# Mamba stage: the scan's decay in PSUM, and B's rows brought by DMA from a DRAM scratch

## The reference

```python
xz = x @ W_in + b_in
x_proj, z = jnp.split(xz, 2, axis=-1)                 # 256 channels each
xa = silu(causal_conv(x_proj, 4 taps) + conv_b)
dtBC = xa @ W_xp + b_xp
dt_int, B_c, C_c = jnp.split(dtBC, [DT_RANK, DT_RANK + D_STATE], axis=-1)   # 16, 16, 16
dt = softplus(dt_int @ W_dt + b_dt)
A = -exp(A_log)
# for each time step t, h of [channel, 16 states], from 0
A_bar = exp(dt_t[..., None] * A)
h = A_bar * h + dt_t[..., None] * B_t[:, None, :] * x_t[..., None]
y_t = sum(C_t[:, None, :] * h, axis=-1)
...
y = (y + xa * D_ssm) * silu(z) @ W_out + b_out
```

## Time and profile before

| | |
|---|---|
| median of three runs | 6530.44 us |
| profiled execution | 6521.4 us |
| its span, first to last instruction | 6519.7 us |
| TensorE's granted clock, mean of the span | 0.909 |
| the Mamba stage's 128 scans | start at 91.3 to 775.7 us |
| busy in 85 to 785 us: scans L2918 on VectorE | 395.1 us, mean 3087 ns |
| the same: drive L2740 on GpSimd | 350.6 us, mean 2747 ns |
| the same: read L2925 on VectorE | 156.2 us, mean 1221 ns |
| the same: decay L2859 on ScalarE | 217.4 us, mean 496 ns |
| the same: copies of B L2851 on ScalarE | 73.9 us, mean 578 ns |

### The profile page before, as it was taken

One profiled execution on the slowest core, in us unless ns is written; L12 is line 12 of the kernel. 1 busy time (PEld: TensorE's weight loads), 2 busy tenths in 40 slices (PEclk: granted clock), 3 DMA queues, 4 the chain that ended last, 5 costly groups with the idle time before them and its releaser, 6 DMA issues. The chain is left out here.

```text
span 6519.7 us, 133036 instructions
## 1 busy us (share of the span) xinstructions
PE 5408.8 (83%) x51329; PEld 3520.5 (54%) x51329; DVE 4462.5 (68%) x7059; ACT 3417.4 (52%) x5825; POOL 2692.6 (41%) x1600
## 2 busy tenths in 40 slices
PE   7889755897789888888888888888888887996866
PEld 4444322454566666665666666666666664663233
DVE  5888889575677767777777777777777775674222
ACT  4565422454556556655566555565556664552123
POOL 2565411000455545554555555555555552660000
PEclk8888866898999999999999999999999998996857
DMA  1000000000000000000000000100010000000000
GB/s 30 0 0 0 4 0 0 6 2 5 28 11 10 25 14 11 10 25 14 10 11 25 15 10 11 28 10 11 11 28 10 12 10 12 2 2 7 12 1 16
DMA packets 69221, 72.82 MB, mean 11 GB/s; under 512 B 20856, under 2 KB 51528, under 8 KB 68048
## 3 DMA queue, kind: packets, MB, share of 16 engines
q1 hardware_dynamic: 60624, 67.88, 4.2%
q10 hardware_dynamic: 8256, 0.03, 0.1%
HBM read 28.06 MB, written 2.10 MB: 5 GB/s over the span
## 5 line engine op out<-in xcount | busy, mean ns | idle before, releaser
L2147 POOL TENSOR_TENSOR lt_qk<-lt_qk,lt_rot 128x1024 f32<-128x1024 f32 x384 | 905.4, 2358 | 560.2 <-DVE lt_rot L2501 560.2
L2157 POOL TENSOR_TENSOR lt_prob<-lt_prob,lt_total 128x1024 f32<-128x1024 f32 x192 | 365.3, 1903 | 1247.4 <-DVE lt_total L2527 1240.6
L2196 PE MATMUL lt_ps<-lt_w_qk,lt_xs 128*128 128x512 f32 x1536 | 773.9, 628 | 74.3 <-issue 52.9
L2152 POOL TENSOR_TENSOR lt_qk<-lt_qk,lt_rnorm 128x1024 f32<-128x1024 f32 x384 | 728.3, 1908 | 58.9 <-ACT lt_rnorm L2375 51.2
L2247 PE MATMUL lt_ps<-lt_z,lt_fold 128*128 128x256 f32 x3072 | 681.0, 380 | 1.1 <-ACT lt_z L2403 1.1
L2368 ACT ACTIVATE lt_sq<-lt_ps 128x1024 f32<-128x1024 f32 x384 | 393.4, 1025 | 521.5 <-PE lt_ps L2196 513.6
L2247 PEld LDWEIGHTS lt_ps<-lt_z,lt_fold 128*128 128x128 f32 x3072 | 585.1, 191 | 122.3 <-ACT lt_z L2403 24.6
L2498 DVE TENSOR_TENSOR lt_qk<-lt_ps,lt_table 128x1024 f32<-128x1024 f32 x384 | 466.1, 1214 | 191.6 <-ACT lt_sq L2368 187.3
L2501 DVE TENSOR_TENSOR lt_rot<-lt_ps,lt_table 128x512 f32<-128x512 f32 x768 | 488.8, 675 | 0.0
L2508 DVE TENSOR_REDUCE lt_norm<-lt_sq 128x16 f32<-128x1024 f32 x384 | 463.7, 1208 | 1.8 <-ACT lt_log L2372 0.3
L2740 POOL TENSOR_TENSOR mb_drive<-mb_u,mb_bs 128x1024 f32<-128x1024 f32 x128 | 350.6, 2747 | 275.8 <-ACT mb_bs L2851 155.6
(11 more groups left out here) (439 smaller groups left out, 11041.0 us busy)
## 6 DMA issues: line engine op xcount, KB each, us to landing
lt_xw<-lt_xw SPq DMA_DIRECT2D x192, 128.0 KB
lt_xs<-h SPq DMA_DIRECT2D x96, 64.0 KB, 1.9
lt_w_qk<-in_L_ffn_Wqkv SPq DMA_DIRECT2D x6, 1024.0 KB, 5.1
lt_xs<-h SPq DMA_DIRECT2D x96, 63.8 KB, 2.0
lt_wvT<-in_L_wvT SPq DMA_DIRECT2D x6, 512.0 KB, 7.2
lt_wo<-in_L_ffn_Wo SPq DMA_DIRECT2D x6, 512.0 KB, 8.3
out<-xo SPq DMA_DIRECT2D x8, 256.0 KB, 2.7
lt_w<-in_L_ffn_W SPq DMA_DIRECT2D x6, 341.0 KB, 3.1
```

The lines of the kernel that those rows point to most:

```text
L2147: pool.tensor_tensor(qk[:, u, :, :], qk[:, u, :, :], rot[:, u % 2, :, :], ALU.add).then_inc(sg["added"], 1)
L2152: pool.tensor_tensor(qk[:, u, :, :], qk[:, u, :, :], rnorm[:, u, :, :].to_broadcast([P, H, DH]), ALU.mult).then_inc(sg["qk"], 1)
L2196: last = pe.matmul(AT[u][:, 512 * k:512 * k + 512], xs[:, m.j, c:c + P], w_qk[:, a, 512 * k:512 * k + 512], start=True, stop=True)
```

## The change

1. `decay` moves from SBUF to PSUM: four of the eight banks. To make room `ps_z` and `ps_c` become one bank, `ps_n` (C's rows) goes from two buffers to one, and `ps_b` goes. Position 0 of each run is zeroed by a memset on VectorE after the layer norm (which now uses decay's banks), and ScalarE waits for it before the first item.
2. B's rows are no longer spread by TensorE and copied by ScalarE. In g = 4 SyncE writes the 16 rows of the next item (`bcd[0:N]`, 16 KB) to a DRAM scratch `mb_rows`, waits, and reads them back with a source that repeats for each of the 128 partitions: first 4 rows (`b_soon`, 512 KB written to SBUF), then 12 (`b_late`, 1536 KB). `bs` now holds a whole item, twice.
3. C's rows are spread in the group that uses them, after the read of the group before (one buffer). The convolution is split over g = 1 and g = 2, z's projection moves from g = 0 to g = 2, and the output's bias on ScalarE from g = 2 to g = 1.

```diff
-    BC = 2 * N
-    assert CT == 2 and BC == 32
+    ROW_C, ROW_DT = 32, 64
+    assert CT == 2 and N <= ROW_C and R <= ROW_C
...
-        bs = sb("bs", [P, 2, 1, 2, S])
-        decay = sb("decay", [P, 2, CT, 2, S])
+        bs = sb("bs", [P, 2, 1, N, S])
+        rows = nc.dram_tensor("mb_rows", [2, N * S], F32).ap()
         drive = sb("drive", [P, 2, CT, 2, S])
...
-        ps_z = psum("ps_z", [P, CT, S])
-        ps_c = psum("ps_c", [P, 2, S])
-        ps_b = psum("ps_b", [P, 2, 1, 2, S])
-        ps_n = psum("ps_n", [P, 2, 1, 2, S])
+        ps_z = psum("ps_z", [P, 2, S])
+        ps_n = psum("ps_n", [P, 1, 2, S])
         ps_y = psum("ps_y", [P, CT * S])
-        ln.ps_mean = ps_b[:, :, 0, :, :].rearrange("p j k s -> p j (k s)")
-        ln.ps_var = ps_n[:, :, 0, :, :].rearrange("p j k s -> p j (k s)")
-        LOADS = 16
+        decay = psum("decay", [P, 2, CT, 2, S])
+        halves = decay[:, :, :, :, :].rearrange("p j t k s -> p j t (k s)")
+        ln.ps_mean, ln.ps_var = halves[:, 0, :, :], halves[:, 1, :, :]
...
+        LOADS = 15
+        SOON = 4
...
+        def run(eng, ahead, here, phase, back):
+
+
+            def item(n, j, more=True):
+                first = isinstance(n, int) and n == 0
+                for g in range(G):
+                    if g < G - 1:
+                        ahead(n, j, g + 1)
+                    elif more:
+                        ahead(n + 1, 1 - j, 0)
+                    here(n, j, g)
+                    if not first:
+                        back(n - 1, 1 - j, g)
+                    if more:
+                        phase(n + 1, 1 - j, g)
+
+            for g in range(G - 1):
+                phase(0, 0, g)
+            ahead(0, 0, 0)
+            pairs(eng, B - 2, item)
+            item(B - 2, 0)
+            item(B - 1, 1, more=False)
+            for g in range(4):
+                back(B - 1, 1, g)
...
+            sp.wait_ge(sg["const"], 4)
+            sp.dma_start(w_xp[:, :, 0:N], w_bc[:, :, R:R + N]).then_inc(sg["w_in"], 16)
...
+            def phase(n, j, g):
+                if g == 4:
+                    sp.wait_ge(sg["bcd"], n + 1)
+                    sp.sem_inc(sg["rows_step"], 1)
+                    if not (isinstance(n, int) and n == 0):
+                        sp.wait_ge(sg["drive"], G * (n - 1) + SOON)
+                        sp.sem_inc(sg["rows_step"], 1)
+                    sp.dma_start(rows[j:j + 1, :].rearrange("a (n s) -> (a n) s", n=N), bcd[0:N, j, :]).then_inc(sg["rows"], 16)
+                    sp.wait_ge(sg["rows"], 16 * (n + 1))
+                    for name, low, high in (("b_soon", 0, SOON), ("b_late", SOON, N)):
+                        sp.dma_start(bs[:, j, 0, low:high, :].rearrange("p n s -> p (n s)"),
+                                     rows[j:j + 1, S * low:S * high].to_broadcast([P, S * (high - low)])).then_inc(sg[name], 16)
+
+            run(sp, idle, idle, phase, idle)
...
-            pool.memset(decay[:, :, :, :, :], 0.0).then_inc(sg["const"], 1)
+            pool.memset(w_xp[:, :, :], 0.0).then_inc(sg["const"], 1)
+            pool.memset(b_xp[:, :], 0.0).then_inc(sg["const"], 1)
...
-                pool.wait_ge(sg["b_copied"], G * n + g + 1)
+                if g == 0:
+                    pool.wait_ge(sg["b_soon"], 16 * (n + 1))
+                if g == SOON // 2:
+                    pool.wait_ge(sg["b_late"], 16 * (n + 1))
                 wait(pool, sg["scanned"], G * n + g - 1)
                 pool.tensor_tensor(drive[:, g % 2, :, :, :], u[:, j, :, :, :].to_broadcast([P, CT, 2, S]),
-                                   bs[:, g % 2, :, :, :].to_broadcast([P, CT, 2, S]), ALU.mult).then_inc(sg["drive"], 1)
+                                   bs[:, j, :, 2 * g:2 * g + 2, :].to_broadcast([P, CT, 2, S]), ALU.mult).then_inc(sg["drive"], 1)
...
-            def ahead(n, j, g):
-                wait(pe, sg["read"], G * n + g - 1)
-                for k in range(2):
-                    last = pe.matmul(ps_n[:, g % 2, 0, k, :], sel[BC:2 * BC, 2 * g + k, :], bcd[BC:2 * BC, j, :], start=True, stop=True,
-                                     tile_position=(BC, 0))
-                last.then_inc(sg["c_spread"], 1)
-
-            def far(n, j, g):
+            def spread(n, j, g):
                 if g == 0:
                     pe.wait_ge(sg["bcd"], n + 1)
-                wait(pe, sg["b_copied"], G * n + g - 1)
+                wait(pe, sg["read"], G * n + g)
                 for k in range(2):
-                    last = pe.matmul(ps_b[:, g % 2, 0, k, :], sel[0:BC, 2 * g + k, :], bcd[0:BC, j, :], start=True, stop=True,
-                                     tile_position=(0, 0))
-                last.then_inc(sg["b_spread"], 1)
+                    last = pe.matmul(ps_n[:, 0, k, :], sel[ROW_C:, 2 * g + k, :], bcd[ROW_C:ROW_C + N, j, :], start=True, stop=True,
+                                     tile_position=(ROW_C, 0))
+                last.then_inc(sg["c_spread"], 1)
...
+                spread(n, j, g)
...
-                    wait(pe, sg["silu_z"], n)
-                    for t in range(CT):
+                if g in (1, 2):
+                    t = g - 1
+                    pe.wait_ge(sg["x"], n + 1)
+                    for k in range(TAPS):
+                        last = pe.matmul(ps_a[:, t, :], taps[:, k, t, :], xpad[:, t, k:k + S], start=(k == 0), stop=(k == TAPS - 1))
+                    last.then_inc(sg["conv"], 1)
+                if g == 2:
+                    wait(pe, sg["biased"], n - 1)
+                    wait(pe, sg["bcd"], n)
+                    for t in range(2):
...
-                if g == 1:
-                    pe.wait_ge(sg["x"], n + 1)
-                    for t in range(CT):
-                        for k in range(TAPS):
-                            last = pe.matmul(ps_a[:, t, :], taps[:, k, t, :], xpad[:, t, k:k + S], start=(k == 0), stop=(k == TAPS - 1))
-                    last.then_inc(sg["conv"], 1)
...
-                    wait(pe, sg["biased"], n - 1)
+                    pe.wait_ge(sg["silu_z"], n + 1)
                     for t in range(CT):
-                        last = pe.matmul(ps_c[0:2 * BC + R, 1, :], w_xp[:, t, :], cz[:, j, t, :], start=(t == 0), stop=(t == CT - 1))
+                        last = pe.matmul(ps_z[0:ROW_DT + R, 1, :], w_xp[:, t, :], cz[:, j, t, :], start=(t == 0), stop=(t == CT - 1))
...
+            act.wait_ge(sg["first_zero"], 1)
...
-            def far(n, j, g):
-                act.wait_ge(sg["b_spread"], G * n + g + 1)
-                wait(act, sg["drive"], G * n + g - 1)
-                act.copy(bs[:, g % 2, 0, :, :], ps_b[:, g % 2, 0, :, :]).then_inc(sg["b_copied"], 1)
...
-                    act.wait_ge(sg["conv"], n + 1)
+                    act.wait_ge(sg["conv"], 2 * n + 2)
...
-                if g == 2:
+                if g == 1:
                     act.wait_ge(sg["out"], n + 1)
                     wait(act, sg["added"], n - 1)
-                    nc.scalar.activation(tmp[:, j, :], ps_c[:, 0, :], ACT.Identity, bias=b_out[:, 0:1]).then_inc(sg["biased"], 1)
+                    nc.scalar.activation(tmp[:, j, :], ps_z[:, 0, :], ACT.Identity, bias=b_out[:, 0:1]).then_inc(sg["biased"], 1)
...
+            dve.wait_ge(sg["ln_log"], B // 2)
+            nc.vector.memset(decay[:, :, :, :, :], 0.0).then_inc(sg["first_zero"], 1)
...
-                                        ps_n[:, g % 2, :, :, :].to_broadcast([P, CT, 2, S]), ALU.mult).then_inc(sg["read"], 1)
+                                        ps_n[:, :, :, :].to_broadcast([P, CT, 2, S]), ALU.mult).then_inc(sg["read"], 1)
```

More of the change, by code:

```diff
@@ L2689, in _ @@
                 sp.dma_start(b_out[:, :], T["L0_attn_b_out"].rearrange("(p a) -> p a", a=1)).then_inc(sg["w_in"], 16)
-                for c in range(2):
-                    sp.dma_start(b_xp[BC * c:BC * c + BC, :], b_bc[R:R + BC, :]).then_inc(sg["w_in"], 16)
-                sp.dma_start(b_xp[2 * BC:, :], b_bc[0:R, :]).then_inc(sg["w_in"], 16)
-        def run(eng, ahead, far, here, phase, back):
-            def item(n, j, more=True):
-                first = isinstance(n, int) and n == 0
-                for g in range(G):
-                    if g < G - 1:
-                        ahead(n, j, g + 1)
-                    elif more:
-                        ahead(n + 1, 1 - j, 0)
-                    if g < G - 2:
-                        far(n, j, g + 2)
-                    elif more:
-                        far(n + 1, 1 - j, g + 2 - G)
-                    here(n, j, g)
-                    if not first:
-                        back(n - 1, 1 - j, g)
-                    if more:
-                        phase(n + 1, 1 - j, g)
-            for g in range(G - 1):
-                phase(0, 0, g)
-            far(0, 0, 0)
-            ahead(0, 0, 0)
-            far(0, 0, 1)
-            pairs(eng, B - 2, item)
-            item(B - 2, 0)
-            item(B - 1, 1, more=False)
-            for g in range(4):
-                back(B - 1, 1, g)
```

(10 more changed lines are left out.)

34 lines of the change are left out of this document (19 added, 15 removed).

## The result

The changed kernel took 6382.88 us in the median (6378.85 to 6385.12, 4 runs), the kernel before beside it 6529.17 us (6524.81 to 6532.07). Its profiled execution took 6383.19 us, its span 6381.5, so profile against profile the gain is 138.2 us.

What follows compares the result with a forecast made beforehand. Mamba is bound by scan and drive excluding each other (groups 5 to 7) and TensorE (groups 0 to 4). 14 x (43.3 - 37.5) = 81, plus 3 and 7, less 2, saves 89 us: 6530.4 - 89 = 6441 us, range 6410 to 6475.

Steps and rivals of the forecast that it cites:

- The exclusion: Mamba groups 5 to 7: VectorE's scan (2.28 us) and GpSimd's drive (2.36) cannot overlap; decay in PSUM ends this.
- The surcharge for a PSUM source: Mamba's scans: by the skill's larger fixed PSUM cost, 128 scans would take 8 us more; left out of the sum.
- the pair of the earlier trace: Layer norm: instructions with a PSUM input (681 ns) and two SBUF inputs (697 ns), taken to show PSUM costs nothing.
- ScalarE into PSUM: Mamba's decay activations: four writes to PSUM taken as 1.70 us as now, between 1.5 and 2.2.
- two cases: Mamba item bounded by TensorE: 36.0 us at full clock, 38.3 to 39.4 if the low level follows its wait; 37.5 taken.
- One sign asked for: Mamba item: TensorE without waits from g = 0 to g = 4 would show the forecast right.
- B's spread: Mamba, TensorE: lies beside C's spread in time, so removing it saves TensorE nothing.
- DMA: Mamba, B's rows: write at most 2.7 us, then 2048 KB in 10.2; both parts hidden, b_late with 7 us to spare.
- The rival of late B: Mamba: the repeated DRAM read is slow, b_late lands 15 us late, items take 51 to 52 us; 6655 us, chance 0.08.
- Ends: Mamba's ends: last item saves 3 us, item 0 saves 7 (3 to 10), 2 lost before the first scan.
- TensorE did not stay slow: Rival in Mamba: TensorE's clock stays low, items take 40 to 41 us; 6485 us, chance 0.18 shared with slow scan.
- the exclusion did not stay: Rival in Mamba: exclusion goes with the scan's instruction, only drives' waits for copies go; 6522 us, chance 0.06.

Runs made afterwards that it cites:

- the six traces named above: Traces of runs with decay in PSUM and the out projection in its old place, group 1; Mamba's pitch 37.06 to 37.52 us an item.
- a shift of 240: Changed kernel with out projection moved to group 5, plus 240 effectless semaphore increments on TensorE ahead of the local transformer: 6671.84 us, ratio 1.0215.
- the shift of the table: Effectless TensorE instructions ahead of the local transformer, 0 to 240, counted from the changed kernel (kernel before stands at 123): 6382.88 to 6671.84 us.
- two runs: Changed kernel with 123 and with 192 effectless increments on TensorE ahead of the local transformer: 6439.59 and 6543.35 us.
- a third: Changed kernel with out projection in group 5, 72 increments ahead of the local transformer and 52 between its two loops: 6368.4 us, ratio 0.9772.

## Why the prediction was wrong, and where it was right

The time was missed by 58 us (6441 against 6382.88). Against the profile, where the working was done, it is 6521.4 - 89 = 6432.4 against 6383.19, so 49.2: 1.2 in Mamba (90.2 saved instead of 89), 47.6 in the local transformer, 0.4 elsewhere. The other 9 us are the distance of the median from the profile, 9.0 before, which I carried over; after, the two agree to 0.3 us.

- *What bounds it, and the scan.* Right. The exclusion came from two SBUF inputs: the scan's median is 2.28 us and its maximum 2.29 (under 2.6 was asked), no drive is over 2.36, and with decay in SBUF all of it comes back. The surcharge for a PSUM source, which I left out, is not there. But the pair of the earlier trace rows was a weak reason for leaving it out: the 681 ns are a subtraction (`cen`) and the 697 ns a multiplication (`h`). And the 8 us that the prediction works out by the Trainium skill's figure, on top of 6441, would make 6449, not 6446.
- *ScalarE into PSUM.* Taken as 1.70 us for four; it is 1.67 (374.20), 462 ns each against 496.
- *TensorE.* 36.0 us at full clock, 38.3 to 39.4 if low clock follows the wait, 37.5 taken; measured 37.33, and 37.06 to 37.52 over the six traces named above. The wait came as laid out, 2.14 us (2.2 foreseen), and the low level did follow it, but only over one sum. So the value was right by a compromise between two cases, and the case was a third; that it came so close is luck. One sign asked for is there: in the item at 392.85 to 419.74 us TensorE has no wait from g = 0 to g = 4.
- *B's spread* "saves TensorE nothing": true of time beside C's spread, which takes 1.06 us alone now (388.19 to 389.25) and 1.07 with B's before. The decay in SBUF run leaves 1.9 us an item to B's rows, the copies and the new order together, which I had not split.
- *DMA.* Write 1.4 us (2.7 allowed), 7.7 for the large part (10.2 for both): hidden, and hidden when doubled. The rival of late B is out. The figures that the prediction takes from the Trainium skill, "DMA: Bandwidth & Descriptors", section on the anatomy of one DMA, are fitted there for transfers that GpSimd issues, and these come from SyncE; the write's 1.4 us are under the fixed 2.0.
- *Ends.* Last item 31.69 us against 33.99, 2.3 saved (3 forecast; in others of the six traces the last item takes as little as 28.6); item 0 from 49.8 to 45.8, 4.0 saved (7 forecast, 3 the lower bound); before the first scan 0.2 won (2 lost forecast: the memset is there, ScalarE waits 3.8 us in its place, but the first scan starts no later). With 14 x 5.98 = 83.7 that is 90.2.
- *The rivals.* TensorE did not stay slow (0.94 where 0.85 was), the exclusion did not stay, B did not come late. None of the three was what happened.

The step that failed is the first sentence of the working: "The change touches the Mamba stage alone, so I read that stage only". It is true of the program's lines and not of its time. The change removes instructions from a queue whose code is loaded in blocks, and everything behind it moves. The long branches were there to be read in the profile before, as idle time with no releaser ahead of the loop's first projection (at the end of the row: idle us, and of it "issue"). Before and after:

```profile
L2196 PE MATMUL lt_ps<-lt_w_qk,lt_xs 128*128 128x512 f32 x1536 | 773.9, 628 | 74.3 <-issue 52.9
```

```profile
L2196 PE MATMUL lt_ps<-lt_w_qk,lt_xs 128*128 128x512 f32 x1536 | 759.1, 617 | 54.9 <-issue 33.2
```

That row says that the stage has something to win or to lose by a shift, though not which. From the 16 items a layer in all six layers, the time from the first item's start to the last's is 3774.2 us before, 3727.8 after and 4000.4 at a shift of 240: the sum lacked a term for this stage, which the runs show from -46 us to +226.

## What to carry to other kernels

Before a forecast that ends with "the rest is unchanged", look at the backward branches of the engine with the most instructions: if some take 0.2 us and others over 3, any edit that changes the number of instructions ahead of the loop can move the time by more than the edit's own worth, and a comparison of two versions should compare that stage too. A gain of a tuned kernel is only attributed once the untouched stages have the same length in both traces, and a few increments of an unused semaphore are a cheap way to test, or to repair, such a placement. And a VectorE instruction that fights with GpSimd's can be freed by moving one of its inputs to PSUM, at no cost in its own time here.

## What the runs showed of the hardware

- A backward branch on TensorE took 0.21 us with its target loaded and 3.3 to 5.1 us without, and each long one came with about nine more 16 KB packets of the instruction queue. Counting the place of each loop over items by the shift of the table (the last layer's plus 141), none was long at the places tried from 0 to 77, a third or half at 123 to 141, all from 173 to 240. Why these are the limits is open.
- After a long branch's 2.9 us of idleness TensorE worked at 1.2 GHz for the next 3.78 us of projection (1.88 at full clock).
- An increment of a semaphore costs TensorE's queue 0.155 us: 10.7 us for 69 of them between two runs, 8.1 us for 52 in a third.
- TENSOR_TENSOR_SCAN on 128x1024 f32 takes 2.28 us from one PSUM and one SBUF input, the same as undisturbed from two SBUF inputs.
- One row of DRAM read by 128 partitions was no obstacle here: 512 KB landed in 4.3 us and 1536 KB in 7.7, some 200 KB per us.
